# Layer norm statistics of the mixer's input: accumulating passes on ScalarE in place of bn_stats on VectorE

## The reference

```
x = x + 0.5 * ffn(layernorm(x));  x = x + mixer(layernorm(x));  x = x + 0.5 * ffn(layernorm(x))
layernorm(x) = (x - mean) / sqrt(var + 1e-5)          # over the 256 features of a token

mixer(x): x_ssm, res = split(x @ W_in.T)              # 512 channels each
  x_conv = silu(causal_conv4(x_ssm) + conv_b);  delta = softplus(x_conv)
  h_t = exp(delta_t * A) * h_(t-1) + x_conv_t**2      # per channel and each of 16 states
  y = (x_conv * sum_n h) * silu(res) + D * x_conv;  return y @ W_out.T
```

## Time and profile before

| | |
|---|---|
| runs | 3700.34, 3705.03, 3710.84 us |
| profiled execution | its page gives the span, 3705.3 us, and no other time |
| VectorE busy | 3111.1 us (84%) |
| ScalarE busy | 2127.6 us (57%) |
| TensorE busy | 2776.9 us (75%) |
| GpSimd busy | 1324.0 us (36%) |
| scans L1187 | 2224.4 us, 512 of 4402 ns |
| decays L1393 | 1018.9 us, 512 of 2004 ns |

### The profile page before, as it was taken

The page is one execution under the profiler, slowest core; times in us unless marked ns, Lnnn a source line. Parts: engine busy times, 40 slices in busy tenths (PEclk is TensorE's granted clock), DMA queues, the critical chain, the costliest instruction groups (busy, mean ns, idle before and its releaser), DMA issues. The chain is left out here.

```text
span 3705.3 us, 29659 instructions
## 1 busy us (share of the span) xinstructions
PE 2776.9 (75%) x9252; PEld 1528.0 (41%) x9252; DVE 3111.1 (84%) x2547; ACT 2127.6 (57%) x2285; POOL 1324.0 (36%) x894
## 2 busy tenths in 40 slices
PE   8702688899889889889979979997896696035553
PEld 4502343354346346435534634543452455024442
DVE  6797579999999999999999999999999667982222
ACT  6300567876877777787687788778767362001111
POOL 0002265446245344534624434460111100035665
PEclk9655799999999899999989999999999896567776
DMA  7202277688678778868877787885686571034667
GB/s 276 106 0 81 78 174 178 144 182 185 150 165 161 178 163 177 191 135 173 179 162 170 158 180 160 177 193 118 127 153 132 113 282 83 0 117 132 218 221 244
DMA packets 146186, 575.75 MB, mean 155 GB/s; under 512 B 22096, under 2 KB 73872, under 8 KB 99216
## 3 DMA queue, kind: packets, MB, share of 16 engines
q0 software_dynamic: 76704, 400.61, 52.1%
q1 hardware_dynamic: 69360, 173.68, 12.7%
HBM read 154.72 MB, written 119.60 MB: 74 GB/s over the span
## 5 line engine op out<-in xcount | busy, mean ns | idle before, releaser
L1187 DVE TENSOR_TENSOR_SCAN state<-state,drive 128x2048 f32<-128x2048 f32 x512 | 2224.4, 4402 | 53.8 <-ACT state L1393 53.6
L1393 ACT ACTIVATE state<-delta,neg_a 128x2048 f32<-128x2048 f32 x512 | 1018.9, 2004 | 213.3 <-DMA delta<-xc 85.5
L1644 PE MATMUL ps_states<-state,ident 128*128 128x512 f32 x1792 | 843.2, 615 | 82.1 <-DMA state<-state 67.1
L1068 POOL DMA_DIRECT2D state<-state x255 | 235.6, 924 | 1299.9 <-DVE state L1187 1289.5
L1546 PE MATMUL ps_proj<-x1t,w_in 128*128 128x512 f32 x1024 | 507.3, 640 | 86.3 <-ACT xc L1342 30.4
L1644 PEld LDWEIGHTS ps_states<-state,ident 128*128 128x128 f32 x1792 | 344.5, 198 | 478.3 <-issue 381.6
L1562 PE MATMUL ps_proj<-conv_in,tap 128*128 128x512 f32 x1024 | 490.9, 631 | 53.6 <-ACT conv_in L1306 32.6
L997 POOL DMA_INDIRECT picked<-normed_rows,slot_now x112 | 356.7, 3185 | 95.0 <-PE ps_rows L1527 49.4
L1013 POOL DMA_INDIRECT x<-routed_rows,row_now x112 | 346.4, 3093 | 34.6 <-issue 34.6
L1546 PEld LDWEIGHTS ps_proj<-x1t,w_in 128*128 128x128 f32 x1024 | 204.2, 204 | 366.8 <-issue 273.2
L1562 PEld LDWEIGHTS ps_proj<-conv_in,tap 128*128 128x128 f32 x1024 | 205.0, 203 | 320.5 <-issue 281.9
(11 more groups left out here) (299 smaller groups left out, 3240.1 us busy)
## 6 DMA issues: line engine op xcount, KB each, us to landing
state<-state POOLq DMA_DIRECT2D x255, 1024.0 KB, 7.0
delta<-xc POOLq DMA_DIRECT2D x24, 1024.0 KB
normed_rows<-rows_in SPq DMA_DIRECT2D x8, 2048.0 KB
x_rows<-x SPq DMA_DIRECT2D x16, 1024.0 KB, 7.7
normed_rows<-rows_mid SPq DMA_DIRECT2D x8, 2048.0 KB
f_total<-x_rows SPq DMA_DIRECT2D x8, 2048.0 KB
routed_rows<-f_routed SPq DMA_DIRECT2D x128, 128.0 KB
out<-f_total SPq DMA_DIRECT2D x8, 2048.0 KB
```

Of the source, the lines that this page charges most:

```text
L1068: nc.gpsimd.dma_start(out=state[held(q)][:], in_=state[held(q - 1)][:], accum_op=ALU.add).then_inc(pair_landed(b, q // 2)[0], 16)
L1187: nc.vector.tensor_tensor_scan(state[held(q)][:], state[held(q)][:], drive[j % 2][:], 0.0, ALU.mult, ALU.add).then_inc(state_ready, 1)
L1393: nc.scalar.activation(state[held(q)][:], delta[j % 2][:], ACT.Exp, scale=g.neg_a[:, j, n:n + 1]).then_inc(decay_ready, 1)
L1644: mm = nc.tensor.matmul(ps_sum[c][:], g.ident[:], state[held(q)][:, c * CH:(c + 1) * CH], start=(opening and n == 1), stop=(n == N - 1))
```

## The change

The statistics of batches 1 to 7 move to ScalarE. It passes over each row twice: `sum_row` (Identity with an accumulating output, the sum of the row) and `sum_spread` (Square with the bias -mean, the sum of squared deviations). Between them `mean_of_rows` multiplies eight sums by -1/256. The passes must write their full output somewhere and use the two `rows_out` tiles as four row buffers; so the first pass of each half waits for `x_in` and also for all `x2_added` of the previous batch. On ScalarE `sum_row` stands in slots 27, 28 and 36, 37, `mean_of_rows` in 29 and 38, `sum_spread` in 29, 30 and 38, 39, and `deviation` in 30 and 39 (before in 32 and 41). In a slot they stand after the copies of projections and output rows and before `soft_log` and `square`. VectorE keeps `scales` after scans 31 and 40, with a tensor_tensor. Batch 0, ahead of the loop, keeps bn_stats on VectorE under new names.

```
+    row_sum, neg_mean, spread_sum = stats[:, :, 0], moments[:, :, 0], moments[:, :, 1]
+    passed_row = [rows_out[i // 2][:, i % 2, :] for i in range(2 * NOUT)]
...
-        def measure(nb, t):
-            if t % TH == 0:
-                dve.wait_ge(x_in[t // TH], nb * 16)
-            nc.vector.bn_stats(stats[:, t, :], x1[:, t, :]).then_inc(stats_done, 1)
-
-        def aggregate(nb, i):
-            dve.wait_ge(stats_done, nb * T + (i + 1) * TH)
...
         def scales(nb, i):
             half = slice(i * TH, (i + 1) * TH)
             dve.wait_ge(rstd_done, 2 * nb + i + 1)
-            dve.wait_ge(moments_done, nb * T + (i + 1) * TH)
-            nc.vector.scalar_tensor_tensor(shift[:, half], moments[:, half, 0], -1.0, rstd[:, half], ALU.mult, ALU.mult
-                                           ).then_inc(shift_done, 1)
+            nc.vector.tensor_tensor(shift[:, half], neg_mean[:, half], rstd[:, half], ALU.mult).then_inc(shift_done, 1)
...
                     for i in range(2):
-                        for t in range(TH):
-                            if q == STATS[i] + t // 4:
-                                measure(b + 1, i * TH + t)
-                        if q == SCALE[i]:
-                            aggregate(b + 1, i)
                         if q == SCALE[i] + 2:
                             scales(b + 1, i)
...
+        def sum_row(nb, t):
+
+            if t % TH == 0:
+                act.wait_ge(x_in[t // TH], nb * 16)
+                for k in range(NOUT):
+                    act.wait_ge(x2_added[k], (nb - 1) * (GO // NOUT) * 16)
+            if t % TH >= 2 * NOUT:
+                act.wait_ge(rows_summed, (nb - 1) * T + t - 2 * NOUT + 1)
+            nc.scalar.activation(passed_row[t % (2 * NOUT)], x1[:, t, :], ACT.Identity, accum_out=row_sum[:, t:t + 1]
+                                 ).then_inc(rows_summed, 1)
+
+        def mean_of_rows(nb, i):
+            half = slice(i * TH, (i + 1) * TH)
+            act.wait_ge(rows_summed, (nb - 1) * T + (i + 1) * TH)
+            act.wait_ge(shift_done, 2 * nb + i - 1)
+            nc.scalar.mul(neg_mean[:, half], row_sum[:, half], -1.0 / D).then_inc(mean_done, 1)
+
+        def sum_spread(nb, t):
+
+            if t % TH == 0:
+                act.wait_ge(mean_done, 2 * (nb - 1) + t // TH + 1)
+            if t % TH >= 2 * NOUT:
+                act.wait_ge(spread_done, (nb - 1) * T + t - 2 * NOUT + 1)
+            nc.scalar.activation(passed_row[t % (2 * NOUT)], x1[:, t, :], ACT.Square, bias=neg_mean[:, t:t + 1],
+                                 accum_out=spread_sum[:, t:t + 1]).then_inc(spread_done, 1)
+
         def deviation(nb, i):
             half = slice(i * TH, (i + 1) * TH)
-            act.wait_ge(moments_done, nb * T + (i + 1) * TH)
+            act.wait_ge(spread_done, (nb - 1) * T + (i + 1) * TH)
             act.wait_ge(normed, count((nb - 2) * T + (i + 1) * TH))
...
                         for i in range(2):
-                            if q == SCALE[i] + 3:
+                            for t in range(TH):
+                                if q == STATS[i] + t // 4:
+                                    sum_row(b + 1, i * TH + t)
+                            if q == STATS[i] + 2:
+                                mean_of_rows(b + 1, i)
+                            for t in range(TH):
+                                if q == STATS[i] + 2 + t // 4:
+                                    sum_spread(b + 1, i * TH + t)
+                            if q == STATS[i] + 3:
                                 deviation(b + 1, i)
```

More of the change, by code:

```diff
@@ L800, in mixer @@
                          "m_normed", "x1_turned", "x1t_copied"))
+    rows_summed, mean_done, spread_done = (sem(n) for n in ("m_rows_summed", "m_mean_done", "m_spread_done"))
     x2_added = [sem(f"x2_added{i}") for i in range(NOUT)]
@@ L1128, in set_rows, with aggregate_early @@
             nc.vector.tensor_copy(row_now[:], g.token_row[:, bass.ds(nb, 1), :].rearrange("p a s -> p (a s)")).then_inc(rows_set, 1)
-        def measure(nb, t):
-            if t % TH == 0:
-                dve.wait_ge(x_in[t // TH], nb * 16)
-            nc.vector.bn_stats(stats[:, t, :], x1[:, t, :]).then_inc(stats_done, 1)
-        def aggregate(nb, i):
-            dve.wait_ge(stats_done, nb * T + (i + 1) * TH)
+        def aggregate_early(i):
+            dve.wait_ge(stats_done, (i + 1) * TH)
             dve.sem_inc(g.passed_dve, 1)
@@ L1139, in aggregate, with scales_early @@
                 nc.vector.bn_aggr(moments[:, t, :], stats[:, t, :]).then_inc(moments_done, 1)
+        def scales_early(i):
+            half = slice(i * TH, (i + 1) * TH)
+            dve.wait_ge(rstd_done, i + 1)
+            dve.wait_ge(moments_done, (i + 1) * TH)
+            nc.vector.scalar_tensor_tensor(shift[:, half], moments[:, half, 0], -1.0, rstd[:, half], ALU.mult, ALU.mult
+                                           ).then_inc(shift_done, 1)
         def scales(nb, i):
@@ L1242, in _ @@
             if p == G2 // 2 - 1:
-                aggregate(0, 0)
+                aggregate_early(0)
             if p == G2 // 2:
-                scales(0, 0)
+                scales_early(0)
             if p == G2 // 2 + 2:
                 copy_early(1)
-        aggregate(0, 1)
+        aggregate_early(1)
         copy_early(3)
-        scales(0, 1)
+        scales_early(1)
         dve.wait_ge(shift_done, 2)
@@ L1278, in read_bank, with deviation_early @@
                                      scale=gate_now[:, s - 1:s]).then_inc(routed_scaled, 1)
+        def sum_row(nb, t):
[8 more added lines that the diff above has]
+        def mean_of_rows(nb, i):
+            half = slice(i * TH, (i + 1) * TH)
+            act.wait_ge(rows_summed, (nb - 1) * T + (i + 1) * TH)
[8 more added lines that the diff above has]
+                                 accum_out=spread_sum[:, t:t + 1]).then_inc(spread_done, 1)
         def deviation(nb, i):
             half = slice(i * TH, (i + 1) * TH)
-            act.wait_ge(moments_done, nb * T + (i + 1) * TH)
+            act.wait_ge(spread_done, (nb - 1) * T + (i + 1) * TH)
             act.wait_ge(normed, count((nb - 2) * T + (i + 1) * TH))
+            nc.scalar.activation(rstd[:, half], spread_sum[:, half], ACT.Ln, bias=eps[:, 0:1], scale=1.0 / D).then_inc(log_done, 1)
+            act.wait_ge(log_done, 2 * nb + i + 1)
+            nc.scalar.activation(rstd[:, half], rstd[:, half], ACT.Exp, scale=-0.5).then_inc(rstd_done, 1)
+        def deviation_early(i):
+            half = slice(i * TH, (i + 1) * TH)
+            act.wait_ge(moments_done, (i + 1) * TH)
             nc.scalar.activation(rstd[:, half], moments[:, half, 1], ACT.Ln, bias=eps[:, 0:1]).then_inc(log_done, 1)
-            act.wait_ge(log_done, 2 * nb + i + 1)
+            act.wait_ge(log_done, i + 1)
             nc.scalar.activation(rstd[:, half], rstd[:, half], ACT.Exp, scale=-0.5).then_inc(rstd_done, 1)
@@ L1460, in copy_early @@
                            ps_rows[i % 2][:].rearrange("p (t k n) -> p t k n", t=2, k=KD)).then_inc(early_copied[0], 1)
-        deviation(0, 0)
+        deviation_early(0)
         act.wait_ge(shift_done, 1)
@@ L1467, in _ @@
         copy_early(2)
-        deviation(0, 1)
+        deviation_early(1)
         act.wait_ge(shift_done, 2)
```

## The result

The changed kernel takes 3791.07 us (3789.51 to 3795.35, 4 runs) against 3703.01 us (3700.34 to 3710.84, 4 runs). The ratio is 1.0243, 95% interval 1.0225 to 1.026: 2.4% slower, 88 us. Forecast: 3794. (The forecast was built on 3705, the median of the three runs shown ahead of it.) The profiled execution has a span of 3793.8 us, 88.5 more than before.

The account below looks back on a forecast made before the run. VectorE sets the body's length, but ScalarE has no lead where the statistics stand. A body costs 9.2 + 4.4 = 13.6 us; 6 x 13.6 + 7 = 89, 3705 + 89 = 3794 us; own range 3765 to 3815, 8 in 10 3748 to 3842.

Parts of the forecast that it names:

- What bounds the kernel: Whole body: VectorE sets its length, busy 301.9 of 310.7 us; ScalarE has no lead exactly where the statistics stand.
- The wait: Slot 27: first sum_row waits for x1 and the previous result's last add, issued at 1515.14, until about 1530 (1527 to 1533).
- rival 2: Slot 27: the result's add lands with x1 at 1522.2; 7 us a body, 49 us, 3754 in all; chance 0.12.
- The price of a pass: ScalarE passes: four sums take 1.6 us, four spreads 2.0, with 0.1 us for each accumulator read-out.
- The 18 us that hung on the read-out: Whole kernel: at the lower pass price, without an accumulator cost, the result would be some 18 us lower.
- First half: Slots 27 to 36: scan 28 starts 12.0 us late, decay 32 9.7, scans 34 to 36 9.2.
- Second half: Slots 36 to 42: ScalarE gains 7.5 us of work, 1.6 and 1.5 hidden, so decay 42 is 4.4 us later.
- Body 0: First body: no result to add, so ScalarE resumes with x1, 8 us sooner; it costs 7 us.
- The sum over bodies: Whole kernel: six bodies at 13.6 us and one at 7 add 89 us to 3705, giving 3794.
- Dear pass: ScalarE passes: each accumulating pass takes 0.7 us; 136 us more, 3841 in all; chance 0.13.
- Quick add: Slot 27: the previous result's add is in with x1, wait ends at 1522.2; 3754 in all; chance 0.12.
- Hidden and faster: Slots 27 to 30: ScalarE's work fits its 9.69 us wait for delta, VectorE's 51 us come off; 3654; chance 0.08.

Follow-up runs that it names:

- experiment 3: Kernel before without bn_stats and bn_aggr in the seven bodies, reusing batch 0's mean and variance, nothing put on ScalarE: 3700.48 us, ratio 0.9985.
- experiment 9: Kernel before, with ScalarE copying the first two chunks of res of unit 3 in slot 31 instead of 32: 3622.30 against 3640.80 us on another chip, ratio 0.9949.
- experiment 1: Changed kernel, but the passes write to picked_t and routed instead of rows_out, so ScalarE waits for x1 alone: 3752.48 us, ratio 1.0126.
- experiment 4: Changed kernel with the same passes but no accumulating outputs, so nothing is summed: 3782.52 us, ratio 1.0206 to the kernel before.
- experiment 7: Changed kernel with the change for the second half alone (slots 36 to 39), first half's statistics on VectorE as before: 3737.15 us, ratio 1.01.
- experiment 5: Changed kernel with only the first half's passes on ScalarE, all in slot 31 before decay 32; second half on VectorE as before: 3706.58 us, ratio 1.0013.

## Why the prediction was right, step by step

**What bounds the kernel.** The reading that decided it, ScalarE's lead slot by slot, was right. The sentence ahead of it, that VectorE sets the body's length, holds only for the average: VectorE was 97% busy, and its work in slots 27 to 40 was worth next to nothing (experiment 3: 6 us of 51). Why ScalarE has no lead there the prediction did not say; experiment 9 shows part of it, TensorE's wait for two copies.

**The wait.** The step that could be read least well from the trace was sized well: I took 15 us from issue to landing, 1530; measured 15.7 by the row that it released, 15.6 in the view of DMA issues. The range of 6.9 to 9.9 us isn't that of all 56 adds, as its heading says: the view by issue had no landing for this one. In the changed kernel the same view has 15.9 at most. Its share in the loss, 6.6 us a body between forecast and rival 2, is 6.8 by experiment 1.

**The price of a pass.** Forecast 1.6 us for four sums and 2.0 for four spreads; measured 1.61 (1558.57 to 1560.18) and 1.98 (0.49 us from one spread to the next). The read-out is 0.19 us long and adds 0.1, as it overlaps its neighbour. The 18 us that hung on the read-out were some 14 by experiment 4. The Trainium skill's figures ("ScalarE: Activation LUTs", section "What ACT_TABLE_LOAD costs") give 399 and 492 ns for the two activations; the trace has 405 and 497. The page has no price for the read-out.

**First half.** The chain from the wait to decay 31 came out as summed, scans 28 and 32 within 1 us. At slot 36 the change was 10.7 us late and not 9.2, and by another path. The prediction let scans 34 to 36 start on their decays, as before. But scans 32 to 35 ran as one block of 17.36 us (row at 1584.23), and scan 36 waited 1.47 us for decay 36, which had waited 1.41 us for a DMA (row at 1603.38). That DMA is the pair add of slots 32 and 33, whose buffer decay 36 takes; it was issued at 1593.83, behind scan 33, 11.4 us late, and landed 9.5 us later. The sum did not have this path.

**Second half.** 3.0 us and not 4.4, and the missing 1.4 is the same wait. TensorE's transposes were 9.3 us late (copy_turned starts 188.7 us into the body, row at 1607.04, against 179.4), decay 36 was 10.7. So the 1.41 us behind the pair add went by where ScalarE would have waited for TensorE. The old wait of 3.05 us has gone whole, 1.6 into the sum passes and 1.4 into the DMA's delay, where I had let it take 1.6. That is why 13.6 forecast and 13.7 measured agree at slot 42 though the two halves of the sum do not: the wait that I left out had no price. That it had none is luck, for the prediction did not look at it. How much of the second half's passes is hidden depends on what comes ahead of them (3.0, 4.3 and 5.4 us in the change and experiments 1 and 7), and I did not take that apart further.

**Body 0.** Forecast 7, measured 7.2 (328.8 against 321.6 us), without an output add to wait for. Experiment 1, where no body waits for one, has 6.9 for b = 3.

**The sum over bodies.** 6 x 13.6 + 7 = 89; in the traces the seven bodies together grew by 91 us, and the runs by 88. Bodies differ: about 324.4 us for b = 2 to 5, but 327.8 for b = 1 and 6; before, b = 2 took 315.9 where b = 1 and 3 to 6 took 310.6 to 311.1. Such extra 3 to 5 us come in one or more bodies of seven of these twelve traces. In b = 2 of the kernel before scan 27 is already 5 us late, so they arise ahead of the statistics; their cause stays open. They add some 7 us to the trace of the change and 5 to that of the kernel before, so they hardly touch the comparison.

**The rivals.** Dear pass: the pass costs 0.40 and 0.50 us, not 0.7. Quick add: 15.7 us, not 7 to 10; its price was right, for experiment 1, where nothing waits for the add, took 3752.48 us where rival 2 gave 3754. The Trainium skill, "DMA: Bandwidth & Descriptors", section "Two DMAs through the same engine are not ordered", says that descriptors of one queue start in order. The trace agrees as far as it goes: the pair add issued ahead, at 1542.25, landed 12.5 us later, at 1554.8, and the output add behind it, at 1558.5. Hidden and faster: the 9.69 us of idle time were real, and experiment 5 puts 8.4 us of passes into them for nothing. The rival failed by place, behind the wait and ahead of decays 28 to 31. Its price, 51 us of gain, was wrong as well: without any statistics the gain is 6 us (experiment 3).

## What to carry to other kernels

Before moving work from a full engine to one that is half idle, lay the two timelines beside each other and read how far the second engine is ahead at just these instructions: an engine that is 76% busy over a body may have no lead in ten slots of it. Even without the wait for the output add, the 14.8 us of work that ScalarE took over in a body (busy for 2231.1 us in place of 2127.6) made the body 6.9 us longer (experiment 1), while VectorE's relief brought at most 1 us (experiment 3). Scratch space is a dependency: here tiles borrowed from a DMA that lands late cost as much as all the work moved, 6.8 of 13.7 us. Where one engine is relieved and nothing gains, follow the wait round to the third engine; here two copies parked behind a DMA wait held TensorE up, and moving them was worth 19 us, where taking all the statistics away was worth 6.

## What the runs showed of the hardware

An accumulating activation on ScalarE is two rows: the activation as long as without it (0.41 us for 128x256 with no operand, 0.50 with one) and a read-out of 0.19 us that overlaps its neighbours and adds about 0.1 (experiment 4). A 256 KB accumulating DMA issued 0.6 us behind a 1 MB one on the same queue took 15.7 us to land, where the adds of this line took 6.9 to 9.9 in the landings that the profile of the kernel before lists. Such a list can leave out just the slow ones: it had no landing for this DMA, and in the changed kernel, where ScalarE waits for it, the same view goes up to 15.9:

```profile
DMA to landing us min/median/max: 7.5/8.6/15.9
```
